# Unit 1's causal triangles: their bias from TensorE goes in batches 1 to 7, and VectorE multiplies the exponentials by ones and zeros

## The reference

```
q, k, v = 16 heads of 8 columns of xn @ Wq, xn @ Wk, xn @ Wv;  q, k = l2norm(q), l2norm(k)
sim  = (q @ k^T) * 8.0
sim  = where(triu(ones(n, n), 1), -max, sim)        # causal: key j > query i is barred
attn = softmax(sim);  o = attn @ v;  result_a = o @ Wo
mixture: top 2 of 8 experts by xn @ Wr, each gelu(xn @ W1[e]^T + b1) @ W2[e]^T + b2, weighted
```

## Time and profile before

| what | value |
|---|---|
| time, median of 3 runs | 667.08 us (666.76 to 668.74) |
| profiled execution: its own time | 667.76 us |
| profiled execution: span from first to last instruction | 666.0 us |
| busy over the span | PE 607.1 us (91%), DVE 461.8 (69%), ACT 450.5 (68%), POOL 427.2 (64%) |
| granted clock of TensorE, mean over the span | 0.971 |
| L813, exponentials | 192 of 1452 ns |
| L666, GpSimd's masks | 256 of 455 ns in the mean of three widths |

### The profile page before, as it was taken

How to read it: one execution, slowest core, us unless ns; L and a number is a source line. 1 busy time by engine, 2 the same in 40 slices (tenths; PEclk the granted TensorE clock), 3 DMA queues, 4 the chain that set the end, 5 groups by cost and what they waited for, 6 DMA issues and landing times.

```text
span 666.0 us, 21498 instructions
## 1 busy us (share of the span) xinstructions
PE 607.1 (91%) x7417; PEld 411.3 (62%) x7417; DVE 461.8 (69%) x1296; ACT 450.5 (68%) x689; POOL 427.2 (64%) x617
## 2 busy tenths in 40 slices
PE   2877468999999989999999999999998999989985
PEld 2756322444444448999999999999994444434432
DVE  6799986677777776444444546777666688868846
ACT  3999546789898984444444444444457988978893
POOL 6356627778888887775600026777655777868773
PEclk9999868999999999999999999999999999989998
DMA  6997684445664568745332334444434466555541
GB/s 172 286 289 243 191 251 107 102 105 122 117 129 112 126 129 218 203 136 145 111 87 71 79 86 107 119 117 115 118 97 75 101 125 135 125 118 111 127 109 48
DMA packets 186593, 89.37 MB, mean 134 GB/s; under 512 B 115456, under 2 KB 176032, under 8 KB 186400
## 3 DMA queue, kind: packets, MB, share of 16 engines
q1 hardware_dynamic: 178192, 70.70, 43.8%
q0 software_dynamic: 8336, 17.84, 9.7%
HBM read 30.17 MB, written 32.24 MB: 94 GB/s over the span
## 4 chain that ended last, share of the span: by engine, by line
PE 74%; issue 4%; DVE 4%; ACT 4%; POOL 3%; DMA 2%; SPq 0%; DVEq 0%; ACTq 0%; POOLq 0%
PE psum L1085 19%; PE psum L1073 18%; PE psum L968 14%; PE psum L883 7%; PE psum L911 7%; ACT prob L813 2%; PE psum L918 2%; PE psum L957 2%; PE psum L979 2%; DMA xt<-xn_cols 2%; POOL prob L666 1%; PE psum L925 1%; POOL rows L650 1%; ACT prob L766 1%; POOL slot_x L652 1%
## 5 line engine op out<-in xcount | busy, mean ns | idle before, releaser
L813 ACT ACTIVATE prob<-psum 128x1536 f32<-128x1536 f32 x192 | 266.9, 1452 | 51.2 <-PE psum L911 47.7
L823 ACT ACTIVATE prob<-psum,prob 128x256 f32<-128x256 f32 x284 | 117.5, 471 | 132.9 <-PE psum L1073 130.1
L650 POOL DMA_INDIRECT rows<-slot_y,idx x128 | 131.4, 1026 | 45.9 <-issue 26.3
L652 POOL DMA_INDIRECT slot_x<-rows,slots x128 | 128.1, 1001 | 35.5 <-issue 29.4
L666 POOL TENSOR_SCALAR_AFFINE_SELECT prob<-prob 128x128 f32<-128x128 f32 (+2 forms) x256 | 112.8, 455 | 42.8 <-ACT prob L813 39.4
L1085 PEld LDWEIGHTS psum<-prob 128*128 128x128 f32 x1136 | 137.8, 192 | 3.6
L968 PE MATMUL psum<-prob,v 128*18 128x448 f32 (+3 forms) x2048 | 132.5, 388 | 7.9 <-POOL prob L666 7.7
L1085 PE MATMUL psum<-prob 128*128 128x128 f32 x1136 | 138.1, 275 | 0.0
L1073 PE MATMUL psum<-xs,prob 128*128 128x256 f32 x568 | 134.8, 380 | 0.9 <-DVE xs L1475 0.8
L1073 PEld LDWEIGHTS psum<-xs,prob 128*128 128x128 f32 x568 | 102.5, 190 | 12.8 <-issue 1.2
L968 PEld LDWEIGHTS psum<-prob,v 128*18 128x18 f32 x2048 | 50.4, 99 | 79.4 <-issue 57.9
(11 more groups left out here) (159 smaller groups left out, 676.5 us busy)
## 6 DMA issues: line engine op xcount, KB each, us to landing
slot_y<-xs SPq DMA_DIRECT2D x71, 128.0 KB
xs<-in_L_attn_x SPq DMA_DIRECT2D x16, 256.0 KB, 4.1
prob<-in_L_ffn_W SPq DMA_DIRECT2D x16, 256.0 KB, 3.6
xn_rows<-prob SPq DMA_DIRECT2D x16, 256.0 KB, 2.6
xn_cols<-xts SPq DMA_DIRECT2D x16, 256.0 KB, 3.0
xt<-xn_cols SPq DMA_DIRECT2D x16, 256.0 KB
rows<-xn_rows SPq DMA_DIRECT2D x16, 256.0 KB, 3.1
out<-acc SPq DMA_DIRECT2D x15, 256.0 KB
```

The lines of the kernel that those rows point to most:

```text
L650: pool.indirect_dma_start(rows[:, j, c, t, :], None, done, where).then_inc(moved[j], 16)
L652: pool.indirect_dma_start(slot_x, where, halves_of_rows[:, j, 0, t, :], None).then_inc(moved[j], 16)
L813: act.activation(prob[:, KEPT[k], :], score[k % 2], ACT.Exp, scale=SCALE / UP ** 2)\
L823: act.activation(hs[:, s, c, :], psum[:, 2 * s + c // 2, (c % 2) * FT:(c % 2 + 1) * FT], ACT.Gelu, bias=ws[:, s, B1C + c:B1C + c + 1]).the ...
```

## The change

In batches 1 to 7 (not in batch 0, and not in the second half) unit 1 gets no bias. TensorE leaves out the two matmuls of L918 there, and the 32 small matmuls start their sums themselves (start=True). ScalarE exponentiates the barred places as well. VectorE then multiplies the 1024 columns of p0 and p1 in prob, in place, by a new tile kept, 128 x 64, of ones and zeros, read 16 times over (clear_triangles). That multiplication stands behind prepare of tile 0 and ahead of evacuate(b-1, 1), waits for exp_done of unit 1, and gives a new semaphore, cleared, for which weigh(b, 0) waits. GpSimd makes kept at the start of the program: one memset and two affine_selects.

```
@@ the constants, on GpSimd @@
+            pool.memset(kept[:], 1.0)
...
             pool.affine_select(out=barred[:], in_=barred[:], compare_op=ALU.is_ge, fill=-60000.0, base=HP,
                                pattern=[[1, HP]], channel_multiplier=-1).then_inc(made, 1)
+            pool.affine_select(out=kept[:], in_=kept[:], compare_op=ALU.is_ge, fill=0.0, base=HP,
+                               pattern=[[1, HP]], channel_multiplier=-1)
...
+            pool.affine_select(out=kept[0:HP, :], in_=kept[0:HP, :], compare_op=ALU.is_ge, fill=0.0, base=0,
+                               pattern=[[1, HP]], channel_multiplier=-1)
@@ scores, on TensorE @@
-            def scores(b, par, k):
+            def scores(b, par, k, unbarred=False):
...
-                    for j in range(2):
+                    for j in range(0 if unbarred else 2):
                         pe.matmul(s[:, j * N:(j + 1) * N], identh[:], bias, start=True, stop=False, skip_group_check=True)
...
-                                               start=False, stop=True, skip_group_check=True)
+                                               start=unbarred, stop=True, skip_group_check=True)
@@ weigh and body, on TensorE @@
+                    if after is not None:
+                        pe.wait_ge(cleared, after)
...
-                    scores(b, par, k)
+                    scores(b, par, k, k == 1 and not second and not known(b, 0))
...
-                        weigh(b, par, 0)
+                        weigh(b, par, 0, None if second or known(b, 0) else b)
@@ VectorE @@
+            def clear_triangles(b):
+
+                dve.wait_ge(exp_done, UN * b + 2)
+                p = prob[:, KEPT[1], 0:2 * N].rearrange("p (a c) -> p a c", c=HP)
+                dve.tensor_tensor(p, p, kept[:].rearrange("p (a c) -> p a c", a=1).broadcast_to([P, 2 * N // HP, HP]),
+                                  ALU.mult).then_inc(cleared, 1)
...
                 if not last:
                     prepare(b + 1, 1 - par, 0, second)
+                if not (second or known(b, 0)):
+                    clear_triangles(b)
                 if not fresh:
                     evacuate(b - 1, 1)
```

More of the change, by code:

```diff
@@ L129, in build @@
         barred = sb("barred", [P, HP], F16)
+        kept = sb("kept", [P, HP])
         back = sb("back", [P, E])
@@ L255, in build @@
         routed = sem("routed")
+        cleared = sem("cleared")
         residue_ready, later_ready = sems("residue_ready later_ready")
@@ L938, in scores, with weigh @@
                 mm.then_inc(scored, 1)
-            def weigh(b, par, c):
+            def weigh(b, par, c, after=None):
                 chunk = CHUNKS[c]
```

## The result

The changed kernel took 674.03 us, median of 9 runs (671.37 to 676.42); the kernel before took 668.17 us beside it (666.76 to 670.78). The ratio is 1.0077, with a 95% interval of 1.0055 to 1.0100: slower, by about 5.1 us, where 2.9 were forecast. The profiled execution took 675.96 us.

A forecast was written before the change was run, and what follows sets the result against it. TensorE was taken as the bound in batches 1 to 7 (busy 128.08 of 130 us). To the 667.1 us median, 2.6 (weigh(b, 1) waits) and 0.3 (constants) were added: 670.0 us; range 666.6 to 672.6.

The forecast's parts named there:

- The removal: Scores 2 on TensorE, held by unit 0's exponential, come only 0.07 us earlier a batch, 0.5 us over seven.
- The multiplication: On VectorE behind tile 0's preparation: 1.23 us, filling idle time and costing nothing on VectorE's own path.
- third rival: The multiplication on VectorE is itself slowed by 0.35 us, weigh(b, 1) is late by 0.72: 672.4 us; chance 0.15.
- The hold-up of GpSimd: Unit 1's mask waits for the two-input multiplication, takes about 1.0 us, ends 0.73 us late; weigh(b, 1) 0.37 late.
- the first rival: GpSimd's masks run beside the multiplication unhindered, only the 0.07 us at scores 2 count: 666.9 us; chance 0.27.
- the 2.6 of the sum: Loss at weigh(b, 1), waiting for unit 2's mask: 0.37 us in each of seven batches, 2.6 us in all.
- The constants: Three small GpSimd instructions ahead of acc's memset at the start delay the first stage: 0 to 0.5 us, taken as 0.3.
- the next batch's unit 0 starts the same game anew: GpSimd catches up before unit 7, so each of batches 1 to 7 repeats the same 0.37 us loss.
- No clock is lost by the new waits: TensorE's granted clock stays at 1.00 despite new waits, as in the last batch, busy 15.77 of 20 us.

The follow-up runs named there:

- e3: Kernel before with unit 1's bias removed in batches 1 to 7, without multiplication, wait or constants; barred places not all zeroed: 669.52 us, 1.0028.
- e4: Changed kernel with a one-input sum over the same 1024 columns in place of the multiplication: 672.9 us, 1.0070.
- e2: Changed kernel run and profiled again without an edit, beside the kernel before: ratio 1.0134.
- e5: Changed kernel with two 8-column matmuls in place of the bias, keeping TensorE's old matmul count: 673.07 us, 1.0069.
- e9: Changed kernel with halved multiplication, later constants, 8-column padding matmuls, and row loads of batches 5 and 6 behind the last transposing DMA: 669.46 us, 1.0007.
- e8: Changed kernel with unit 1's bias kept on TensorE beside the multiplication and its wait, constants made later: 673.42 us, 1.0065.
- e12: Changed kernel, but unit 0 loses its bias; halved multiplication ahead of tile 0, 8-column padding, late constants, moved row loads: 667.52 us, 0.9993.
- e6: Kernel before with unit 1's bias replaced by two 8-column matmuls in batches 1 to 7, no multiplication, wait or constants: 671.7 us, 1.0038.

## Why the prediction was wrong

The sign and the mechanism were right; the size was not, and the time lay above the range.

**The removal** was read rightly: 0.40 us of idle time ahead of scores 2, released by ScalarE, and 0.07 to 0.1 us a batch in e3.

**The multiplication** took 1216 to 1394 ns, median 1221, for the 1.23 us worked out. By the source view of its line:

```profile
L1419 DVE TENSOR_TENSOR prob<-prob,kept x7: 1216/1221/1394, 123.9 to 238.3; 128x1024 f32<-128x1024 f32 x7
```

It wasn't slowed (third rival out), but for once, 1394 ns in batch 1, where the mask started within 0.01 us of it and took its usual 0.30 us. Its time on VectorE costs nothing (e4).

**The hold-up of GpSimd** came as forecast, with the mask at 0.81 to 0.86 us in six batches and held until 0.14 us after the multiplication, which excludes the first rival. (It was forecast at about 1.0 us; it started 0.17 us later against the batch's first exponential than before, and ended 0.08 us earlier than forecast.) e4 shows that the second input does it. weigh(b, 1) was 0.30 us late in batch 4 where 0.37 was forecast, and batches 3 and 4 grew by 0.24 and 0.32. The exponential of unit 5, which comes behind weigh(b, 1), was 0.23 to 0.34 us later in each of the seven batches, 1.9 us in all, for the 2.6 of the sum: the term was about a third too high. Batch 7's 0.23 us don't show in the table, as its row, with the expert tiles, is as long as before (274.11 us for 274.13).

**The constants** cost 0.49 us at the first normalisation, the upper bound, where I took 0.3. Whether all of it reaches batch 0 is less sure: its first exponential started at 91.1 to 92.0 us, mean 91.43, in the four profiles with the three instructions at the start (after, e2, e4, e5), and at 90.5 to 91.6, mean 91.02, in the other ten.

**The step that failed** is this: "the next batch's unit 0 starts the same game anew, since all of this is counted from the exponential of unit 0", and with it that the sum had no term outside these waits. Two things were left out.

First, the seven batches don't only repeat one wait. The change moved VectorE's copies against GpSimd's masks at the end of a batch too, and a copy that had started 0.18 us ahead of a mask started behind it. Through the transposing DMA this held up the first scores of batches 6 and 7: 1.4 us in the profile after, 1.2 us in e2 (0.84 and 0.33). e9 shows the cause, by taking the load out of the DMA's way. Batches 1 and 2 grew by 0.3 us each beyond the wait at weigh(b, 1) as well, at L1054 and at the start of batch 3; what makes these two isn't shown.

Second, TensorE executes 14 matmuls and 14 weight loads less, and in the second half, 300 us behind the last changed instruction, it stops for 1.3 to 1.6 us in a place where none of the ten other profiles stops. The waits of TensorE after, 500 to 640 us:

```profile
PE psum L932 <- issue: 1.3, 1, 1.3
...
PE psum L925 <- ACT prob L820: 0.7, 1, 0.7
```

The 0.7 us in the second row are at a batch's start again, that of batch 12; some kernels have them (e5, e8) and some don't (e9, e12). In e4 the profile puts a wait of 1.0 us in this place down to the transposing DMA; the cause of its lateness stays open.

Together: 0.5 (constants) + 3.7 (batches 1 to 7: 1.9 at weigh(b, 1), 1.4 at the starts of batches 6 and 7, 0.4 in the rest) + 1.3 (the stop in the second half) = 5.5 us, beside 5.1 by the ratio, whose interval is 3.7 to 6.7 us. The match says less than it seems to. The same program gave 1.0134 in another comparison, 9 us. And the two profiled spans differ by 8.2 us: the other 2.7 lie mostly in batch 0 (1.1), which scatters by as much as 2.8, and in batches 11 and 12 (0.9). How often the clock falls can be a part of what makes medians of one program differ, as said at e6; the rest was not found.

**"No clock is lost by the new waits"** held for the waits of the seven batches (1.00 and 0.99 granted), but not for the stop in the second half in each execution. In e3, 544 to 546 us, behind the 1.59 us:

```profile
544.00:546.00 2.00, 2.00 (x23) 0.51 (x13) 0.32 (x1) 2.00 (x2) 0.44 (x2) 0.55 0.00 0
```

0.55 granted is near the lower level, 1.2 GHz, and a project of two matmuls took 1.50 us there for 0.91 (the row of 544.01 above). In the profile after, behind 1.28 us, the clock stayed at 1.00.

## What to carry to other kernels

Two inputs in SBUF on VectorE cost next to nothing on VectorE here and something on GpSimd: before such an instruction is put into idle time, look at what GpSimd has to do in it, and whether a form with one input or a split in two will do. Where a change is worth tenths of a microsecond a batch, list the close races (a copy 0.2 us ahead of a mask, a transfer that lands just in time), since each is a term of its own once everything moves. And if an engine's program changes its length, look at code that wasn't touched: a wait for "issue" in the middle of small matmuls was worth 1.3 us here, beside the 1.9 of the seven waits.

## What the runs showed of the hardware

The hold-up of GpSimd isn't confined to its masks. In e8 the indirect DMA of L659 (0.97 us in the kernel before) took 1.75 us in four batches and ended at 183.03 in batch 4, 0.84 us after the multiplication's end at 182.19; in batches 1, 2 and 7 it took 1.9 to 2.0 us, with the same distance to the end. With one input instead (e4) the DMA that met the sum's end took 0.97 us. The Trainium skill ("SBUF — State Buffer", section Who interferes with whom) infers that a TENSOR_TENSOR leaves the making of descriptors alone; here it doesn't leave this DMA alone, which reads its slots from SBUF besides, and which of the two is held up isn't separated. For the masks its rule, that the one that comes second stands still, is what six of the seven batches after show (0.81 to 0.86 us for 0.30 to 0.34); in batch 1, where both started at once, it was the multiplication that took longer (1.39 us) and the mask took 0.30.

The hold-up goes the other way as well: a COPY of 128x256 f16 on VectorE that started 0.04 us behind a mask on GpSimd took 0.58 us for 0.22.
